# A graph layer's edge stage: a gather waits for the sums three groups back instead of seven

## The chip, the core and the metric

The kernel runs on one core of a Trainium2 chip. Its engines are TensorE (PE in the profile; PEld is its weight load), VectorE (DVE), ScalarE (ACT), GpSimd (POOL) and SyncE (SP). Each runs its own list of instructions in order, and they meet only at semaphores. The metric is device time of one execution in microseconds (us).

## What is computed

A graph attention layer and a mixture of eight experts, one behind the other, over 2500 nodes of 512 features. The change touches only the first. Cut to what matters:

```python
# nodes: layernorm of x; 40000 edges (src, dst), sorted by dst
h = nodes @ W + b_w                        # 2500 x 512
s_dst, s_src = h @ a[:512], h @ a[512:]
e = leaky_relu(s_dst[dst] + s_src[src] + b_a, 0.2)
w = exp(e)
denom = segment_sum(w, dst)
out = segment_sum((w / denom[dst])[:, None] * h[src], dst)
x = x + out                                # then the experts
```

## The kernel before

**Stages.** First `h` is made and stored to a table in DRAM (`node_table`), a row of 516 f32 for each node: two halves of features, a one (which sums to the denominator) and the node's score. Then comes the edge stage, which this case is about, from about 92 to 574 us of the profile. Then come the second layernorm, the routing and the experts.

**The edge stage.** The 40000 edges are cut into chunks of 128 (an edge on each partition), and four chunks are a group: 79 groups, numbered here from 0 to 78, the last with one chunk. As edges are sorted by target, a group's targets nearly always lie in one tile of 128 nodes; where they reach into a second tile the group has an *extra*, a second pass for that tile. 19 of the 79 groups have one: 3, 7, 11 and so on up to 71, then 76. A group goes through these steps:

1. POOL issues four indirect DMAs (L506), one for each chunk, which fetch 128 rows of the table into slot `g % 8` of the ring `rows`.
2. ACT waits for all four (`got`) and for DVE to have read the low exponentials before, and makes eight activations of 128x128 (L951): `E`, and a second set in PSUM.
3. DVE takes the larger of the two (`Wt`, L1217, after the short `lane`, L1222) and masks it in four instructions into `S` (L1228), which releases the semaphore `S_ok`. Then, in its own program order, it adds the finished sums of group g-2 to `acc` (L1235), for which it waits for `agg_ok`.
4. PE multiplies `S` with `rows` (L705, function `sums`), 16 matmul records of 128x257 for a full group; the last one raises `agg_ok`. The PSUM banks alternate between two groups.
5. An extra repeats steps 2 to 4 from the same slot: ACT follows at once with another eight activations (`E`, `E2x`), DVE weighs them behind its add of group g-2, and PE sums them behind the group's own sums. They do not raise `agg_ok` but a semaphore of their own.

PE, ACT and DVE run this in a loop of eight groups (`RING`) with branches around the extras; at the loop's edge they load the words that tell a group's tiles. POOL's list is written out for all 79 groups. `S` has four slots of its own, `rows` eight.

**What the change touches.** `gather(g)` on POOL. POOL has nothing else to do from the first gather to the last, and nothing follows on it until `acc_ok`, the end of the stage.

Of the kernel before, what the change touches and what calls it, by code (L numbers as in the profile page):

```python
# [20 lines left out]
def gnn_moe_kernel(nc, x, src, dst, gnn_W, gnn_b_w, gnn_a, gnn_b_a, Wg, bg, W1, b1, W2, b2, out):  # L21
# [7 lines left out]
    CJ = -(-CH // P)  # L29
    GC = 4  # L30
    RING = 8
    U = 4
    NG = -(-CH // GC)
    GC_LAST = CH - GC * (NG - 1)
    NGR = -(-NG // RING) * RING
    SR = U
    BACK = 2
# [20 lines left out]
    with ExitStack() as ctx:  # L58
# [3 lines left out]
        def sem(name):  # L62
            return ctx.enter_context(nc.semaphore(name))
# [23 lines left out]
        def sg(name, shape, dt, into=None):  # L87
            top[0] += size(shape, dt)
            return (into or ctx).enter_context(nc.sbuf_tensor(name, shape, dt))
# [17 lines left out]
        top[0] = ring  # L107
        rows = sg("rows", [P, RING, GC, ROW], F32, first)
        assert layer_end <= top[0]
# [160 lines left out]
        st_row = [[sem(f"st_row{s}{j}") for j in range(2)] for s in range(2)]  # L270
        got = [sem(f"got{r}") for r in range(RING)]
        exp_ok, id_ok = sem("exp_ok"), sem("id_ok")
        max_ok = [sem("max_ok0"), sem("max_ok1")]
        S_ok, agg_ok = sem("S_ok"), sem("agg_ok")
# [76 lines left out]

        def window_words(eng, regs, i, back=0, each=RING):

            eng.load(regs, window[0:1, bass.ds(each * i + BACK - back, len(regs))])
# [133 lines left out]
        def _(pool):  # L488
# [11 lines left out]

            def gather(g):

                if g >= RING - 1:
                    pool.wait_ge(agg_ok, g - RING + 2)
                for c in range(GC if g < NG - 1 else GC_LAST):
                    nc.gpsimd.indirect_dma_start(  # L506
                        out=rows[:, g % RING, c, :], out_offset=None, in_=table,
                        in_offset=bass.IndirectOffsetOnAxis(ap=srcT[:, GC * g + c:GC * g + c + 1], axis=0))\
                        .then_inc(got[g % RING], 16)
# [5 lines left out]
            for g in range(NG):  # L515
                gather(g)
# [574 lines left out]
        def _(dve):  # L1091
            regs = [dve.alloc_register(f"dve_window{k}") for k in range(U + BACK)]
            n_dv = [0]
# [121 lines left out]
            def largest(q, n=GC):  # L1215

                return nc.vector.scalar_tensor_tensor(out=Wt[:, q, 0:n, :], in0=E1[:, q, 0:n, :], scalar=FINITE,  # L1217
                                                      in1=(E2x[:, 0, 0:n, :] if q == 2 else ps_E2[:, 0:n, :]), op0=ALU.min, op1=ALU.max)
# [6 lines left out]
            def masked(q, w, n=GC):  # L1225

                for c in range(n):
                    m = nc.vector.scalar_tensor_tensor(  # L1228
                        out=S[:, w, c, :], in0=ps_id[:, :], scalar=lane[:, w, c:c + 1],
                        in1=Wt[:, q, c, :], op0=ALU.is_equal, op1=ALU.mult)  # L1230
                return m
# [43 lines left out]
            def step_of_group(g, r, i, first=False, chunks=GC):  # L1275

                word, word_before = dve.snap(regs[r + BACK]), dve.snap(regs[r])
                dve.wait_ge(exp_ok, g + 1)
                if not (first and r < 2):
                    dve.wait_ge(S_ok, g - 1)  # L1280
                tile = dve.snap(tile_in(word))
                lanes(r % SR, g, tile)
                largest(r % 2, chunks).then_inc(max_ok[r % 2], 1)
                dve.wait_ge(max_ok[r % 2], U // 2 * i + r // 2 + 2)
                masked(r % 2, r % SR, chunks).then_inc(S_ok, 1)
                if not (first and r < 2):
                    add_group(g - 2, r % 2, word_before, first and r < 3)
                extras(g, None if first and r < 2 else g - 1, word, chunks)
# [17 lines left out]
            dve.wait_ge(edges_ok, 2)  # L1306
            window_words(dve, regs, 0, BACK, U)
            for r in range(U):
                step_of_group(r, r, 0, first=True)
            with dve.Fori(1, NG // U) as i:  # L1310
                window_words(dve, regs, i, BACK, U)
# [248 lines left out]
```

## Time and profile before

| | us |
|---|---|
| three runs | 866.72, 867.32, 867.40 |
| median | 867.32 |
| span of the profiled execution | 861.7 |
| what lies around the span, against the median | 5.6 |
| edge stage within the span | about 92 to 574 |

The span runs from the first to the last instruction of the profiled execution. Busy time of an engine is the time that its instructions take, without register and semaphore work. The granted clock (PEclk) is 1.00 when TensorE runs at 2.4 GHz and 0.50 at 1.2 GHz.

### The profile page before, as it was taken

What the parts mean: (1) busy time and instruction counts of PE and PEld (TensorE: products, weight loads), DVE (VectorE), ACT (ScalarE), POOL (GpSimd) and SP (SyncE); (2) the same over time, 40 slices, a digit from 0 to 9 for tenths busy, and PEclk for the clock granted to TensorE, in tenths of its full rate; (3) what the DMA queues carried; (4) which work ended last, traced back from release to release, by engine and by line L of the source; (5) the groups of instructions that cost most, each with busy time, mean ns of one, the idle gap of its engine ahead of it and who ended that gap; (6) DMA issues with size and microseconds to landing.
All of it is one profiled execution on the core that took longest, in us unless ns stands there. A gap on an engine that the chain in (4) does not pass through costs nothing.

```text
span 861.7 us, 14833 instructions
## 1 busy us (share of the span) xinstructions
PE 696.6 (81%) x3260; PEld 553.6 (64%) x3261; DVE 457.2 (53%) x1232; ACT 415.4 (48%) x1134; POOL 457.3 (53%) x530
## 2 busy tenths in 40 slices
PE   4999355879888787879788888959889999999960
PEld 3777245657766666667676767845547787888840
DVE  5998223555555555556465555668485433333320
ACT  4443442545545554536455545618754444545430
POOL 5000575666666666666666666310105677777750
PEclk9999687998989899989999898988988999999995
DMA  5342576666666666666656666407993577777768
GB/s 197 117 155 92 156 213 164 172 188 168 186 181 174 178 177 182 186 171 183 189 166 184 176 179 179 118 27 283 334 380 127 104 131 131 135 131 135 130 91 250
DMA packets 58299, 146.96 MB, mean 171 GB/s; under 512 B 8868, under 2 KB 18708, under 8 KB 57880
## 3 DMA queue, kind: packets, MB, share of 16 engines
q0 software_dynamic: 35216, 106.84, 50.6%
q1 hardware_dynamic: 22968, 37.16, 12.3%
q10 hardware_dynamic: 80, 2.56, 1.0%
q8 instruction: 14, 0.23, 0.1%
q14 instruction: 21, 0.17, 0.1%
HBM read 118.17 MB, written 33.47 MB: 176 GB/s over the span
## 4 chain that ended last, share of the span: by engine, by line
PE 40%; issue 19%; DVE 11%; DMA 11%; ACT 4%; POOL 4%; POOLq 2%; DVEq 2%; another core or an unknown queue 2%; ACTq 1%; SPq 1%
PE ps L705 30%; DMA result<-y,si 8%; PE ps L659 3%; POOL rows L506 2%; DMA x_all<-in_x_dram 2%; ACT E L951 2%; ACT ps L951 2%; PE ps L844 1%; DVE Wt L1217 1%; PE ps L785 1%; DVE S L1228 1%; DVE acc L1235 1%; PE ps L755 1%; POOL xg L593 1%
## 5 line engine op out<-in xcount | busy, mean ns | idle before, releaser
L705 PE MATMUL ps<-rows,S 128*128 128x257 f32 x1556 | 383.4, 404 | 98.7 <-issue 83.9
L506 POOL DMA_INDIRECT rows<-node_table,srcT x313 | 301.8, 964 | 234.4 <-issue 83.8
L705 PEld LDWEIGHTS ps<-rows,S 128*128 128x128 f32 x1556 | 312.3, 202 | 169.6 <-issue 121.3
L951 ACT ACTIVATE E<-sdst_b,rows 128x128 f32 x389 | 124.0, 389 | 236.2 <-DVE Wt L1217 120.7
L1235 DVE TENSOR_TENSOR acc<-acc,ps 128x514 f32 x99 | 68.0, 687 | 116.1 <-remote 77.6
L1228 DVE SCALAR_TENSOR_TENSOR S<-ps,lane,Wt 128x128 f32<-128x128 f32 x389 | 109.6, 345 | 4.4 <-issue 0.8
L951 ACT ACTIVATE ps<-sdst_b,rows 128x128 f32 x313 | 96.2, 351 | 2.0 <-issue 2.0
L844 PE MATMUL ps<-W_e,xgT 128*128 x352 | 83.4, 380 | 0.0
L602 POOL DMA_INDIRECT result<-y,si x44 | 70.4, 1601 | 11.4 <-issue 7.1
L1222 DVE TENSOR_TENSOR lane<-dstT,node_id 128x4 f32 (+1 forms) x98 | 16.1, 164 | 111.5 <-issue 77.0
L844 PEld LDWEIGHTS ps<-W_e,xgT 128*128 128x128 f32 x352 | 63.4, 190 | 6.9
L659 PE MATMUL ps<-Wb,xT 128*128 128x512 f32 x240 | 59.1, 403 | 2.5 <-DVE dstT L1184 1.4
L858 PE MATMUL ps<-W_hi,hidT 128*128 x176 | 55.6, 437 | 3.0 <-DVE hidT L1512 2.8
L1058 ACT ACTIVATE act_h<-hid 128x256 f32<-128x256 f32 x44 | 18.4, 418 | 77.2 <-DVE hid L1519 67.2
L1529 DVE TENSOR_TENSOR y_b<-ps,b_b 128x512 f32<-128x512 f32 x44 | 30.4, 692 | 46.4 <-PE ps L858 39.4
L659 PEld LDWEIGHTS ps<-Wb,xT 128*128 128x128 f32 x240 | 45.6, 194 | 12.6 <-DVE dstT L1184 1.6
L1217 DVE SCALAR_TENSOR_TENSOR Wt<-E,ps 128x512 f32<-128x512 f32 (+1 forms) x79 | 53.3, 675 | 0.0
L593 POOL DMA_INDIRECT xg<-xn_table,gi x44 | 48.1, 1094 | 8.1 <-issue 4.6
L1519 DVE TENSOR_TENSOR hid<-ps,b_b 128x256 f32<-128x256 f32 x44 | 18.7, 424 | 55.1 <-PE ps L844 51.3
L551 POOL COPY si<-dst_row 128x1 int32 (+1 forms) x45 | 31.9, 709 | 19.0 <-DVE need L1503 11.9
L858 PEld LDWEIGHTS ps<-W_hi,hidT 128*128 128x128 f32 x176 | 32.6, 188 | 11.8 <-issue 5.9
L548 POOL COPY gi<-src_row 128x1 int32 (+1 forms) x45 | 9.7, 215 | 54.0 <-DVE src_row L1458 35.9
(203 smaller groups left out, 678.8 us busy)
## 6 DMA issues: line engine op xcount, KB each, us to landing
W_e<-in_L_ffn_W_dram SPq DMA_DIRECT2D x16, 512.0 KB, 8.5
node_table<-rows SPq DMA_DIRECT2D x20, 258.0 KB, 2.7
result<-acc SPq DMA_DIRECT2D x20, 256.0 KB, 2.5
xn_table<-xn SPq DMA_DIRECT2D x20, 256.0 KB, 2.2
rows<-node_table,srcT POOLq DMA_INDIRECT x313
x_all<-in_x_dram SPq DMA_DIRECT2D x19, 256.0 KB, 3.1
out_dram<-result SPq DMA_DIRECT2D x1, 2500.0 KB, 16.7
out_dram<-result ACTq DMA_DIRECT2D x1, 2500.0 KB, 18.4
```

The costliest lines, as they stand in the source:

```text
L506: nc.gpsimd.indirect_dma_start(out=rows[:, g % RING, c, :], out_offset=None, in_=table, in_offset=bass.IndirectOffsetOnAxis(ap=srcT[:, GC ...
L551: nc.gpsimd.tensor_copy(si[:, r, :], dst_row[:, bass.ds(i, 1)]).then_inc(si_ok, 1)
L593: nc.gpsimd.indirect_dma_start(out=xg[:, r, :], out_offset=None, in_=xn_table, in_offset=bass.IndirectOffsetOnAxis(ap=gi[:, r, :], axis=0) ...
L602: nc.gpsimd.indirect_dma_start(out=result, out_offset=bass.IndirectOffsetOnAxis(ap=si[:, (r - LAG) % YR, :], axis=0), in_=y[:, (r - LAG) % ...
L659: m = pe.matmul(ps_h[s][j][:, :], xT[:, s, a, k, j * P:(j + 1) * P], Wb[:, b, k, :], start=(n == 0), stop=(n == 3 * KT - 1))
L705: m = pe.matmul(ps_agg[q][:, a, 0:HALF], S[:, w, c, :], rows[:, r, c, a * HALF:(a + 1) * HALF], start=(c == 0), stop=(c == n - 1))
L844: m = pe.matmul(ps_hid[1 - s][:, 0:F], xgT[:, 1 - s, k * P:(k + 1) * P], W1_e[:, bass.ds(e, 1), k, :].rearrange("p e f -> p (e f)"), start ...
L858: m = pe.matmul(ps_y[s][:, :], hidT[:, s, a, k * P:(k + 1) * P], W[:, bass.ds(e, 1), k, :].rearrange("p e d -> p (e d)"), start=(c == 0), ...
L951: m = nc.scalar.activation(e[:, c, :], sdst_b[:, bass.ds(tile * P, P)], ACT.Exp, bias=bias, scale=scale)
L1217: return nc.vector.scalar_tensor_tensor(out=Wt[:, q, 0:n, :], in0=E1[:, q, 0:n, :], scalar=FINITE, in1=(E2x[:, 0, 0:n, :] if q == 2 else p ...
L1228: m = nc.vector.scalar_tensor_tensor(out=S[:, w, c, :], in0=ps_id[:, :], scalar=lane[:, w, c:c + 1], in1=Wt[:, q, c, :], op0=ALU.is_equal, ...
L1235: nc.vector.tensor_tensor(a, a, ps_agg[q][:, :, 0:HALF], ALU.add).then_inc(count, 1)
```

## The change

A new constant `AHEAD = 3`, and the wait ahead of a gather. Before, the gather of group g waited until the sums of groups 0 to g-7 were done; now it waits for those of groups 0 to g-3, and it does so from group 3 on instead of from group 7. The ring keeps its eight slots; no instruction is added or taken out apart from four more waits (groups 3 to 6), and nothing else changes.

```diff
     GC = 4
     RING = 8
+    AHEAD = 3
@@
             def gather(g):
 
-                if g >= RING - 1:
-                    pool.wait_ge(agg_ok, g - RING + 2)
+                if g >= AHEAD:
+                    pool.wait_ge(agg_ok, g - AHEAD + 1)
                 for c in range(GC if g < NG - 1 else GC_LAST):
```

## Rows read from the trace of the kernel before

**Rows 1.** The page: costliest group; count, busy us, mean ns, idle before

```profile
L705 PE MATMUL ps<-rows,S 128*128 128x257 f32 x1556 | 383.4, 404 | 98.7 <-issue 83.9
```

**Rows 2.** Waits, 150 to 550 us: who for whom, total us, times, longest

```profile
PE ps L705 <- issue: 62.1, 69, 2.4
...
PE ps L705 <- DVE acc L1235: 2.6, 4, 0.8
```

**Rows 3.** Windows: POOL's gathers, then DVE's `Wt` instructions, up to a time

```profile
92.00:343.40 251.40, 164.98 (x172) 0.88 0.66 180
...
92.00:344.40 252.40, 32.74 (x48) 0.89 0.66 181
```

**Rows 4.** Timeline of POOL at 343 us: start, us, idle before

```profile
343.44 0.94 POOL L506 DMA_INDIRECT rows<-node_table,srcT  x1 [1.26 <-remote]
```

**Rows 5.** Timeline of DVE: `Wt` of groups 7, 47 (and its extra), 48 and 71

```profile
157.16 0.68 DVE L1217 SCALAR_TENSOR_TENSOR Wt<-E,ps 128x512 f32<-128x512 f32 x1
...
391.54 0.68 DVE L1217 SCALAR_TENSOR_TENSOR Wt<-E,ps 128x512 f32<-128x512 f32 x1
...
395.37 0.69 DVE L1217 SCALAR_TENSOR_TENSOR Wt<-E,E2x 128x512 f32<-128x512 f32 x1
396.09 1.13 DVE L1228 SCALAR_TENSOR_TENSOR S<-ps,lane,Wt 128x128 f32<-128x128 f32 x4
...
399.28 0.68 DVE L1217 SCALAR_TENSOR_TENSOR Wt<-E,ps 128x512 f32<-128x512 f32 x1
...
533.23 0.68 DVE L1217 SCALAR_TENSOR_TENSOR Wt<-E,ps 128x512 f32<-128x512 f32 x1
```

**Rows 6.** Timeline of the stage's start, groups 0 and 1

```profile
92.24 1.15 POOL L506 DMA_INDIRECT rows<-node_table,srcT  x1 [78.54 <-DMA node_table<-rows]
...
97.47 0.94 POOL L506 DMA_INDIRECT rows<-node_table,srcT  x1 [0.30 <-issue]
...
104.71 8.80 PE L705 MATMUL ps<-rows,S 128*128 128x257 f32 x32 [15.06 <-issue]
...
105.15 1.28 ACT L951 ACTIVATE E<-sdst_b,rows 128x128 f32 x4 [2.65 <-DMA rows<-node_table,srcT]
...
107.85 0.68 DVE L1217 SCALAR_TENSOR_TENSOR Wt<-E,ps 128x512 f32<-128x512 f32 x1
```

**Rows 7.** Timeline of POOL: the gather that sums released

```profile
296.25 0.94 POOL L506 DMA_INDIRECT rows<-node_table,srcT  x1 [1.35 <-PE ps L705]
```

**Rows 8.** Windows, L705 alone: PE and PEld busy (records), clock, DMA share, GB/s

```profile
294.88:295.30 0.42, 0.42 (x2) 0.33 (x1) 0.50 0.77 177
200.20:241.00 40.80, 33.58 (x149) 27.86 (x148) 1.00 0.68 184
357.80:404.90 47.10, 39.86 (x160) 32.14 (x160) 0.93 0.66 180
...
379.83:388.60 8.77, 5.64 (x17) 4.03 (x16) 0.81 0.60 168
392.17:395.60 3.43, 3.43 (x17) 3.00 (x16) 1.00 0.75 181
```

**Rows 9.** Timeline, 382 to 384 us: PE and DVE

```profile
382.71 0.38 PE L705 MATMUL ps<-rows,S 128*128 128x257 f32 x1 [1.73 <-issue]
383.43 0.16 DVE L1222 TENSOR_TENSOR lane<-dstT,node_id 128x4 f32 x1 [6.12 <-issue]
```

**Rows 10.** Windows, L705 alone: blocks of groups 3 and 7, and 72 to 78

```profile
137.90:143.70 5.80, 5.77 (x17) 4.77 (x18) 0.64 0.63 162
...
159.85:163.50 3.65, 3.65 (x18) 3.21 (x18) 1.00 0.75 213
...
541.20:571.80 30.60, 29.33 (x134) 24.95 (x133) 1.00 0.24 69
```

**Rows 11.** DMA queues, 200 to 500 us: packets, MB, share

```profile
q0 software_dynamic: 16264, 53.69, 65.5%
q14 instruction: 1, 0.01, 0.0%
```

## The prediction

> **What bounds the kernel now.** I read the page first. TensorE's edge matmuls are its costliest group, 1556 records and 383.4 us busy, all in the edge stage [rows 1]. Then the waits: from 150 to 550 us the PE idles 62.1 us on "issue" in 69 pieces of at most 2.4 us, and 2.6 us on DVE; it never waits for rows to land [rows 2]. "Issue" means that its own list of instructions came slowly, which I come back to. So the PE and the pace of its instructions set the stage.
>
> How far ahead do gathers run? Up to 343.40 us POOL had issued 172 gathers, which is groups 0 to 42, and up to 344.40 DVE had made 48 `Wt`, which is groups 0 to 38 and nine extras [rows 3]. The first gather of group 43 starts at 343.44 [rows 4], when the PE, which follows DVE, can be on group 38 at most. A block (the 16 records of a group or an extra) takes 3.4 us at full clock [rows 8]. Under the new rule this gather would wait for the sums of group 40. So the wait will bind for each group; the change does what it says.
>
> The period: `Wt` of group 7 starts at 157.16 and that of group 71 at 533.23 [rows 5]. Eight loops of eight groups take 376.07 us, 47.0 each. In such a loop there are ten blocks, 160 records, which occupy the PE for 39.9 of 47.1 us [rows 8].
>
> **The change, part by part.** Nothing is added that costs by itself: a wait on POOL, behind which only POOL's later gathers stand, and POOL has 5.2 us of issuing for a group (92.24 to 97.47) [rows 6] against 47.0 / 8 = 5.9 now. What changes is that data no longer lies ready when ACT wants it. A chain closes: sums of g-3, gather of g, landing, exponentials, `Wt`, mask, sums of g. Its pieces:
>
> *From the first gather to the end of the sums.* At the start of the stage nothing lies ready and the trace shows just this. Group 1: gather at 97.47, ACT starts at 105.15 after waiting for the rows, `Wt` at 107.85, and the PE row of groups 0 and 1 ends at 104.71 + 8.80 = 113.51 [rows 6]. That is 16.0 us: 7.7 to the landing, 2.7 for ACT, 5.7 for mask and sums.
>
> *From the end of the sums to the next gather.* The one plain case: POOL at 296.25 after an idle of 1.35 that the PE ended [rows 7]. The block's last record begins at 294.9 and lasts to 295.3, as the short window with two records around it shows [rows 8]. So 0.98 us. The chain from sums to sums three groups on is 17.0 us, 5.67 a group. By itself this is less than 5.9.
>
> *The extra.* It stands every fourth group, between the sums of groups 3 and 4, 7 and 8, and so on. Since its rows are those of its group, its work starts at once and can't be spread. Take group 47: `Wt` at 391.54, the extra's `Wt` at 395.37, its mask done at 396.09 + 1.13 = 397.22, 5.68 after the group's own `Wt` [rows 5]. The group's sums end 5.66 after its `Wt` (113.51 - 107.85), so the extra's sums can't start sooner than these end; two blocks of 3.5 with their starts make 7.3 us from the sums of group 3 to those of group 4. At the loop's edge DVE sets it: `Wt` of 47 to `Wt` of 48 is 399.28 - 391.54 = 7.74 us [rows 5].
>
> Four groups then cost one chain and one extra, not four thirds of a chain: from the sums of 0 by the chain to those of 3 (17.0), and by the extra to those of 4 (7.3 or 7.7). Eight groups: 34.0 + 7.3 + 7.7 = 49.0 us, against 47.0 now. This is the floor of the new period, 2.0 us above the old with nothing else in it. The old one holds slow stretches as well.
>
> *The slow stretches.* The block of group 44 takes 8.77 us with 16 records of its own (the seventeenth is the end of the block before), the block of group 46 takes 3.43 [rows 8]. At 382.71 one record comes 1.73 us after the one before; DVE's `lane` of group 45 comes after 6.12 us of "issue" in the same stretch [rows 9]. Such a block comes once in each loop, at the group that is 4 past a multiple of eight, and then some smaller ones. Group 4 of a loop is on the new chain, right behind an extra, where the PE has no slack to hide it. What is it worth? Nothing if an idle PE lets the list of instructions catch up; up to 12 us if the smaller ones land on the chain too (47.1 - 10 x 3.5 = 12 us is all that the PE loses in a loop now). I take the one long block in full, 8.8 - 3.4 = 5.4, as it starts on both engines when neither was waiting, and the smaller ones as hidden. The period becomes 54.4 us, 7.4 more. Eight loops: +59 us.
>
> Here the Trainium skill has a rule, in "Runtime: NRT & Kernel Launch", section "Instruction fetch mechanics": the list of instructions is fetched in order in blocks, and a taken branch whose target isn't in the two blocks held makes the engine wait for a fetch by DMA. By it the stretches belong to places in the loop and stay, which gives the sum above; a catch-up during waits would give the first rival's. The trace bears it out in part: the places do recur, but from 200 to 500 us the instruction queues show one packet against 16264 of the gathers [rows 11], so no fetch by DMA is seen at each of them.
>
> *The ends of the stage.* At the start, the sums of group 3 end at 143.3 at the earliest (from 137.90 16 records at mixed clock) [rows 10]; group 6 then starts its gather at 144.3 and group 7, behind the sums of 4 (a block of 3.5 and an extra of 3.5 later), at 151.3, so its sums end at 167.3. They end at 163.5 now [rows 10]: +4. At the stage's end, groups 72 to 78 now take 571.8 - 541.2 = 30.6 us behind the sums of 71 [rows 10]. By the chain: extra and 72 (7.3), 73 (3.5), the chain to 76 (17.0), extra and 77 (7.3), and 1 for the short 78: 36. So +6. Together +10.
>
> After the stage nothing is different: POOL's next work already waited for `acc_ok`.
>
> **Sum.** 59 + 10 = +69 us. The profiled span of 861.7 becomes 931; the median stands 5.6 above the span, so 867.3 becomes 936 us.
>
> **Rivals.**
>
> A, *the slow stretches vanish in the waits.* For it: most of these stretches are short, and the PE will pause ahead of most blocks. Against it: the long one comes right behind an extra, where neither PE nor DVE would be waiting. Then the period is 49.0: 8 x 2.0 + 10 = +26, 893 us.
>
> B, *the clock falls.* The PE would be busy 35 of 54 us, with a pause of about 2 us ahead of most blocks. The block of 44 had a clock of 0.81, but from 200.20 to 241.00 it is 1.00 throughout, with 40.8 - 33.6 = 7.2 us of pauses in between [rows 8]. If it falls in half the six blocks on the chain of a loop (0, 3, 4, 7 and two extras), each adds 3.4: +10 a loop, +80 in all, 1016 us.
>
> The Trainium skill speaks for B, in "TensorE: Matmul & The Clock Gate", section "HAM oscillation": short bursts of matmuls, each behind a wait for a DMA, run at the low clock again and again. By it the time would go towards 1016; the clock of 1.00 over 40 us with pauses in it disagrees so far, but there the pauses are rarer than they will be.
>
> C, *faster: fewer gathers ahead ease the slow stretches for everyone.* The gathers' queue has a share of 65.5% [rows 11] and could be what slows the engines' lists. If they vanish with it and the chain is shortened too, time is gained. It decides where the chain falls below 16.0 us (then 32.0 + 15.0 = 47.0). At 15.0 the period is 45.0: -16 + 10 = -6, 861 us. Against it: of the 7.7 to the landing, 4 are POOL's issuing of four gathers, which doesn't shrink, and group 1 was measured where just one group was ahead of it. At about 15.8 the whole would come to no change.
>
> **How the numbers follow.** About 0.2% (1.7 us) is what a measurement of this kernel can tell. Chances: the forecast 0.61 (its own range 915 to 989: from half the long block, 49.0 + 2.7, to all 12 us on the chain, 61.0), A 0.20, B 0.12, C 0.07, of which 0.04 faster and 0.03 the same. Slower 0.93. The range of 8 in 10 runs from 888, just under A, to 990: it leaves out C and most of B.
>
> **What the profile after would show.** POOL before the first gather of each group idle, released by the PE; ACT's `E` waiting for DMA or "remote" where it now waits for DVE; PE waits between blocks of about 2 us; `Wt` to `Wt` over eight groups 54 us (49 would be A, over 60 B, 47 or less C); at groups 4 of a loop still a block of 8 to 9 us; the stages behind 574 us shifted and otherwise equal. The prediction would be wrong if a gather lands much sooner than 7.7 us after its issue, if the extra overlaps with the next group more than DVE's order allows, or if the slow stretches move or multiply when the engines run in step.

## The result and the profile after

| us | before | with the change |
|---|---|---|
| median | 867.36 (4 runs) | 878.06 (4 runs, 876.02 to 879.09) |
| ratio | | 1.0112, 95% interval 1.0097 to 1.0127 |
| span of the profiled execution | 861.7 | 877.4 |

The change makes the kernel 1.1% slower, 10.7 us. The forecast was 69 us, with 888 to 990 as its range; the direction was right and the size was not. One point on the time itself: the profiled execution after took 879.09 us for its span of 877.4, so 1.7 us lie around a span, not 5.6. The profiled execution of before was therefore some 4 us quicker than its median, and the two profiles differ by 15.7 us where the medians differ by 10.7.

The page after, the two costliest groups of the edge stage (against [rows 1]; lines are one higher in the changed file):

```profile
L706 PE MATMUL ps<-rows,S 128*128 128x257 f32 x1556 | 377.2, 402 | 122.2 <-DVE acc L1236 74.1
L507 POOL DMA_INDIRECT rows<-node_table,srcT x313 | 298.6, 954 | 266.7 <-PE ps L706 93.1
```

POOL now waits for the PE, as the change asks. The PE waits more than before and for another reason. Waits of the PE, 150 to 570 us, against [rows 2]:

```profile
PE ps L706 <- DVE acc L1236: 68.3, 33, 3.4
PE ps L706 <- issue: 20.2, 10, 3.0
PE ps L706 <- DVE S L1229: 5.6, 3, 2.9
```

"Issue" falls from 62.1 to 20.2 us and DVE rises from 2.6 to 73.9. (These are waits for `S`, as the mask's semaphore and that of the add stand side by side ahead of a block.) The label "issue" needs care here: in both of these traces many semaphore events are not recorded (the experiments come back to it), and an idle time whose end has no event goes to "issue". A measure that needs no semaphore is the idle time inside a block, between two of its 16 records, where the PE waits for nobody. Pieces of over 0.3 us, counted in the trace from `Wt` of group 7 to that of group 71, add up to 45.9 us before (51 pieces) and to nothing after. So the slow stretches of the PE are gone: the block of group 44, which took 8.77 us with 16 records [rows 8], now looks like any other. The blocks at this place of the eight loops (groups 12, 20 and so on to 68) took 8.8 to 11.4 us before and take 3.6 to 3.7 after. Windows, L706 alone; the columns are those of [rows 8]; the blocks of groups 39, 44 and 51, then most of the stage:

```profile
349.05:352.70 3.65, 3.57 (x17) 3.15 (x18) 1.00 0.69 186
...
380.10:383.70 3.60, 3.60 (x17) 2.85 (x16) 1.00 0.73 193
423.35:429.70 6.35, 6.29 (x16) 5.07 (x17) 0.54 0.60 166
150.00:550.00 400.00, 308.94 (x1284) 253.59 (x1284) 0.94 0.61 169
```

The block of group 51 ran at a clock of 0.54 and took 6.3 us: rival B, in single blocks.

The period, from the timeline of DVE, `Wt` of groups 7 and 71, against [rows 5]:

```profile
148.39 0.68 DVE L1218 SCALAR_TENSOR_TENSOR Wt<-E,ps 128x512 f32<-128x512 f32 x1
...
546.74 0.68 DVE L1218 SCALAR_TENSOR_TENSOR Wt<-E,ps 128x512 f32<-128x512 f32 x1
```

398.35 / 8 = 49.8 us a loop, against 47.0. So the 15.7 us of the spans are: group 7 comes 8.8 us sooner (157.16 to 148.39), eight loops cost 22.3 more, and about 2 are left for the end of the edge stage and all behind it.

The chain that the forecast wrote down, in the timeline of all engines from 335 to 374 us: group 39 with its extra, group 40, then the gathers of 42 and 43 and the block of 43:

```profile
335.84 0.94 POOL L507 DMA_INDIRECT rows<-node_table,srcT  x1 [2.02 <-PE ps L706]
...
343.75 1.28 ACT L952 ACTIVATE E<-sdst_b,rows 128x128 f32 x4 [4.56 <-DMA rows<-node_table,srcT]
...
346.55 0.68 DVE L1218 SCALAR_TENSOR_TENSOR Wt<-E,ps 128x512 f32<-128x512 f32 x1
...
349.13 10.66 PE L706 MATMUL ps<-rows,S 128*128 128x257 f32 x48 [3.26 <-DVE acc L1236]
...
353.72 0.94 POOL L507 DMA_INDIRECT rows<-node_table,srcT  x1 [1.37 <-PE ps L706]
...
360.06 0.94 POOL L507 DMA_INDIRECT rows<-node_table,srcT  x1 [1.65 <-PE ps L706]
...
373.11 8.06 PE L706 MATMUL ps<-rows,S 128*128 128x257 f32 x36 [0.84 <-DVE acc L1236]
```

From gather to the end of the sums: 7.9 to the landing, 2.8 to `Wt`, 2.6 to the first record, 3.7 for the block, 17.0 in all where the forecast had 16.0. The release is shorter than forecast where POOL is ready: the 48 records (group, extra, group 40) end at 359.79 and the gather of 43 starts at 360.06, 0.3 us later. The gather of 42 comes about 1 us behind the sums of 39, as forecast. In e6, the same kernel on another chip, the release is 0.27 us behind most groups and the chain 17.0 to 17.4 us where the clock stays up; there the two errors nearly cancel.

### The profile page after: what moved, and what is told of

It reads as the page before. It is cut to its first block, busy times and chain, and to the rows that moved or that the text cites. A ratio compares the mean times of both kernels' runs of the same rounds, so it can differ in the third digit from the quotient of the medians.

```text
span 877.4 us, 14833 instructions
## 1 busy us (share of the span) xinstructions
PE 688.0 (78%) x3260; PEld 549.3 (63%) x3261; DVE 453.8 (52%) x1232; ACT 415.5 (47%) x1134; POOL 454.1 (52%) x530
## 3 DMA queue, kind: packets, MB, share of 16 engines
q0 software_dynamic: 35216, 106.84, 48.5%
## 4 chain that ended last, share of the span: by engine, by line
PE 33%; issue 18%; DVE 14%; DMA 12%; POOL 10%; ACT 5%; DVEq 2%; POOLq 1%; another core or an unknown queue 1%; ACTq 1%; SPq 1%
PE ps L706 15%; POOL rows L507 9%; PE ps L845 6%; DMA rows<-node_table,srcT 5%; PE ps L859 4%; DMA result<-y,si 3%; PE ps L660 3%; ACT ps L952 2%; DVE acc L1236 2%; DVE S L1229 2%; ACT E L952 2%; DVE Wt L1218 2%; DMA x_all<-in_x_dram 2%; DMA xg<-xn_table,gi 2%; PE ps L835 2%
## 5 line engine op out<-in xcount | busy, mean ns | idle before, releaser
L706 PE MATMUL ps<-rows,S 128*128 128x257 f32 x1556 | 377.2, 402 | 122.2 <-DVE acc L1236 74.1
L507 POOL DMA_INDIRECT rows<-node_table,srcT x313 | 298.6, 954 | 266.7 <-PE ps L706 93.1
L706 PEld LDWEIGHTS ps<-rows,S 128*128 128x128 f32 x1556 | 309.1, 202 | 190.1 <-DVE S L1229 92.8
L594 POOL DMA_INDIRECT xg<-xn_table,gi x44 | 48.1, 1094 | 8.1 <-issue 5.5
L1520 DVE TENSOR_TENSOR hid<-ps,b_b 128x256 f32<-128x256 f32 x44 | 18.7, 424 | 50.7 <-PE ps L845 47.3
```

The costliest lines, as they stand in the source:

```text
L507: nc.gpsimd.indirect_dma_start(out=rows[:, g % RING, c, :], out_offset=None, in_=table, in_offset=bass.IndirectOffsetOnAxis(ap=srcT[:, GC ...
L594: nc.gpsimd.indirect_dma_start(out=xg[:, r, :], out_offset=None, in_=xn_table, in_offset=bass.IndirectOffsetOnAxis(ap=gi[:, r, :], axis=0) ...
L706: m = pe.matmul(ps_agg[q][:, a, 0:HALF], S[:, w, c, :], rows[:, r, c, a * HALF:(a + 1) * HALF], start=(c == 0), stop=(c == n - 1))
```

## The experiments

The kernel before does not take the same time everywhere, and that turned out to be the main finding. The experiments ran in five sets, each on another chip, with the kernel before beside them; its medians were 787.6, 786.9, 868.6, 862.2 and 865.0 us, and within a set its times agree within 1%. So each run must be read against the kernel before of its own set. The text speaks of two kinds of chip, with and without slow stretches. As no chip served twice, and that of the first measurement isn't on record, it isn't shown that the chip is the cause and not something else that differed from set to set.

The loop time is that from `Wt` of group 7 to `Wt` of group 71, divided by eight, in the timeline of DVE of each run. "Idle in blocks" is the measure from above, for the same eight loops. "Signals" tells how many of the landing signals of the gathers the trace recorded: each gather raises its semaphore in 16 steps, however many rows it fetches, so 313 gathers make 5008 and 103 make 1648. e3, e4, e5, e7, e8, e10, e12 and e14 are one execution each.

| run | before beside it | time | `Wt` of 7 | loop, us | idle in blocks, us | signals |
|---|---|---|---|---|---|---|
| before (first profile) | | 867.36 | 157.16 | 47.0 | 45.9 | 1295 of 5008 |
| the change (first profile) | 867.36 | 878.06 | 148.39 | 49.8 | 0 | 2120 of 5008 |
| e1, four ahead | 787.58 | 788.03 | 140.65 | 40.0 | 0 | 5008 of 5008 |
| e2, five ahead | 787.58 | 787.73 | 138.66 | 40.1 | 0 | 5008 of 5008 |
| e3, one gather of four | 787.58 | 749.82 | 139.45 | 35.6 | 0 | 1648 of 1648 |
| e4, half of the PE's sums | 787.58 | 785.81 | 139.55 | 40.0 | 0 | 5008 of 5008 |
| e5, before again | 786.87 | 789.56 | 139.84 | 40.1 | 0 | 5008 of 5008 |
| e6, the change again | 786.87 | 880.76 | 151.65 | 49.4 | 0 | 5008 of 5008 |
| e7, two ahead | 786.87 | 1146.43 | 166.47 | 77.7 | 0 | 5008 of 5008 |
| e8, the change, one gather of four | 868.63 | 809.51 | 151.71 | 41.1 | 0 | 1389 of 1648 |
| e9, four ahead again | 868.63 | 860.33 | 144.01 | 47.8 | 21.0 | 1382 of 5008 |
| e10, one gather of four again | 868.63 | 763.50 | 154.02 | 35.6 | 0 | 1290 of 1648 |
| e11, a pause on POOL | 862.15 | 873.02 | 158.43 | 48.3 | 30.0 | 1627 of 5008 |
| e12, half of the PE's sums again | 862.15 | 861.48 | 157.33 | 47.6 | 0 | 1278 of 5008 |
| e13, five ahead again | 862.15 | 857.74 | 147.67 | 47.0 | 44.2 | 1367 of 5008 |
| e14, a quarter of the rows | 864.96 | 867.27 | 161.10 | 47.0 | 51.4 | 906 of 5008 |
| e15, four ahead, then seven | 864.96 | 864.31 | 142.77 | 49.0 | 42.6 | 1325 of 5008 |

The last column divides the runs as the time of the kernel before does: where it takes 787 us every signal is recorded, where it takes 860 to 870 us it is 18% to 84% of them. In the second kind the labels "issue" and "remote" ("remote": a release whose origin the profile doesn't show) are therefore rough. It also names a rival to all theories below, which no run tests: every time on record comes with a span and a granted clock, so from an execution that was recorded, and the recording itself may be what holds the engines up on these chips.

The theories: 1, the slow stretches come where PE and DVE run without waiting, and waits hide them; 2, they come with long unbroken runs of POOL's gathers; 3, the forecast's, they belong to places in the code and stay.

### e1 and e2: four and five groups ahead

```diff
-    AHEAD = 3
+    AHEAD = 4        # e2: 5
```

> A gather waits for the sums four groups back instead of three. The chain from sums to sums (17.0 us) then covers four groups, and a loop of eight groups costs at least two chains and, one group further, an extra: 2 x 17.0 + 7.5 / 5 x 8 is under 42 us, so POOL's issuing sets the floor, 8 x 5.0 to 5.2 = 40 to 42 us a loop. Theory 1 (the slow stretches come where PE and DVE run through their lists without having to wait; a wait lets the lists catch up): PE is busy 35 of 42 us and still waits, so few stretches, 42 to 44 us a loop, 30 to 40 us faster than the kernel before. Theory 2 (the stretches come at the end of long unbroken runs of POOL's indirect DMAs, 8 to 12 in a row, and end when POOL pauses): the runs are as long as in the kernel before, the stretches are back, 46 to 48 us a loop, within 8 us of the kernel before. Theory 3 (they belong to places in the loop's code, as in the prediction): also 46 to 48 us.

> A gather waits for the sums five groups back. The chain does not bind. Theory 1: like the kernel before in steady state, since data lies ready again: 46 to 47 us a loop, within 5 us of before, perhaps a few us gained at the start of the stage. Theory 2: the same as before, within 5 us. Theory 3: the same. This run is the middle of the series 3, 4, 5, 7 and shows where the time turns.

Ratios to the kernel before of the set: 1.0011 (0.9988 to 1.0034) and 0.9996 (0.9981 to 1.0012). The loop is 40 us, but so it is for the kernel before (e5): there are no slow stretches on this chip. The expectations about them are untested here. What both runs do show is that from four groups on the chain does not bind: POOL's issuing sets the pace, as the floor of 40 to 42 us said.

### e3 and e4: light gathers, light PE

```diff
# e3: from group 8 on only chunk 0 is gathered
-                for c in range(GC if g < NG - 1 else GC_LAST):
+                for c in range(GC if g < RING else 1):
# e4: the PE sums two chunks of four
+                n = min(n, 2)
                 for c in range(n):
```

In e3 ACT's wait on `got` counts to match.

> The kernel before, but from group 8 on only the first of the four chunks of a group is gathered; the other three keep the rows of eight groups earlier. It leaves out three quarters of the gathers. ACT, DVE and PE do all their work, and nothing waits for data. Theory 1 (stretches where PE and DVE never wait) and theory 3 (places in the code): the stretches stay, the period of eight groups stays at 45 to 47 us. Theory 2 (unbroken runs of POOL's indirect DMAs, or their traffic): the stretches vanish and the period falls to the PE's own, 10 blocks of 3.5 us plus the loop's edge, 37 to 39 us, 60 to 80 us faster in all.

> The kernel before, but the PE sums only the first two of four chunks of each group and extra, so a block takes 1.7 instead of 3.5 us. It leaves out half of the sums. POOL then sets the pace with unbroken runs of gathers, and ACT, DVE and PE wait for data. Theory 1: no stretches, 40 to 42 us a loop. Theory 2: the runs of indirect DMAs are longer than ever, so PE, DVE and ACT show instructions 0.7 us apart through most of the stage, and POOL itself is slowed: 46 us a loop or more. Theory 3: the stretches stay where they were but are partly hidden: 42 to 44 us.

Without stretches to see, these tell the bounds: with half of the PE's work the loop stays at 40.0 us, with a quarter of the gathers it falls to 35.6, the PE's own ten blocks. So POOL bounds the kernel before on such a chip.

### e5 and e6: both kernels again, side by side

> The kernel before, unchanged, for its profile beside the next run. In the last call the kernel before took 787.6 us on its chip, 80 us less than in the first measurement, and the changed variants there showed no slow stretch on the PE at all. Theory 4: the slow stretches are a matter of the chip or of its surroundings, not of the kernel's code (against theory 3) and not of unbroken runs of indirect DMAs alone (against theory 2). Where the time is near 787, the trace has no stretch of PE or DVE instructions 0.7 us apart outside the extras, and POOL issues without a pause, a group each 5.0 us, 40 us a loop; where it is near 867, it looks like the first trace, 47 us a loop.

> The change, unchanged. The chain of the prediction (two chains of 17.0 and two extras of 7.3 and 7.7 us: 49.0 us a loop; 48.0 to 48.3 measured where the clock did not fall) does not depend on slow stretches. On a chip without them the kernel before has 40 us a loop, so the change costs 8 us a loop and about 8 at the end, nothing at the start: +65 to +80 us, 855 to 870 us, against 787 before; the changed kernel is then nearly as fast as on the first chip (878), as the stretches had left it anyway. On a chip with them: 876 to 880 against 867, as first measured. Rival (the change helps or costs the same everywhere): a ratio of 1.01 on any chip.

Here the change costs 12%: 880.76 against 786.87, ratio 1.1203 (1.1170 to 1.1236), 94 us, more than the 65 to 80 expected. Between the two profiles lie 91.7 us: 75.0 are the eight loops (9.4 each, where the expectation had 8), 5 come behind them, and 11.8 stand ahead of group 7, where "nothing at the start" was expected: the chain binds there too, from group 3 on. The kernel before, `Wt` of groups 7 and 71 and its waits from 150 to 450 us:

```profile
139.84 0.68 DVE L1217 SCALAR_TENSOR_TENSOR Wt<-E,ps 128x512 f32<-128x512 f32 x1
...
460.33 0.68 DVE L1217 SCALAR_TENSOR_TENSOR Wt<-E,ps 128x512 f32<-128x512 f32 x1
...
ACT E L951 <- DMA rows<-node_table,srcT: 74.3, 38, 3.5
POOL rows L506 <- issue: 73.4, 241, 0.3
```

POOL never waits for anything but its own next issue (at most 0.3 us), and ACT waits for rows, where in the first profile data lay ready. The changed kernel:

```profile
151.65 0.68 DVE L1218 SCALAR_TENSOR_TENSOR Wt<-E,ps 128x512 f32<-128x512 f32 x1
...
547.07 0.68 DVE L1218 SCALAR_TENSOR_TENSOR Wt<-E,ps 128x512 f32<-128x512 f32 x1
```

Its loop of 49.4 is within 0.4 of the first profile's 49.8. So the changed kernel is the same on both kinds of chip, set by the chain, and the kernel before is the one that differs, 40.1 or 47.0. The small first ratio is a difference of two losses. The rival of e6, a ratio of 1.01 everywhere, is refuted, and so far theory 4 of the expectation to e5 holds.

### e7: two groups ahead

```diff
-    AHEAD = 3
+    AHEAD = 2
```

> A gather waits for the sums two groups back. The same chain of 17.0 us then covers two groups. Four groups cost two chains, or one extra edge and one and a half chains, whichever is longer: 34.0 us or 7.5 + 25.5 = 33.0, so 68 us a loop against 48 to 49 with three. That is 79/8 x 19 = +190 us against the change: about 1050 to 1070 us. Rival (the landing gets much shorter when fewer gathers are under way): under 60 us a loop, under 990 us.

The chain's direction and more: 77.7 us a loop, 1146 us. Of the 9.7 us beyond 68, the clock is the one cause that shows. The window of the PE's edge matmuls, columns as in [rows 8]:

```profile
150.00:750.00 600.00, 345.57 (x1229) 280.40 (x1229) 0.75 0.39 109
```

A mean clock of 0.75, against 0.94 with three ahead. In the timeline of the PE four blocks of each loop take longer than the usual 3.65 us, together by 8.5 to 10.1 us, which is nearly the whole of the 9.7. The wait of the next gather is long enough here for the clock to fall again and again. That is rival B, true at two groups and a minor matter at three. The Trainium skill's rule of "TensorE: Matmul & The Clock Gate", section "HAM oscillation", describes this run; at three groups it was too strong.

### e8: the change with light gathers

The edit of e3 on the changed kernel.

> The change, but from group 8 on only the first of the four chunks of a group is gathered; the other three keep older rows. It leaves out three quarters of the gathers. It tests a term of the chain: of the 16.0 us from the first issue to the end of the sums, 3 x 1.25 = 3.75 are the issuing of three more gathers on POOL. By the chain, a loop falls from 48.1 (24.07 for four groups, as measured) to 2 x (17.0 - 3.75 + 7.1) = 40.7 us, or a little more where the clock falls. Total on a chip without slow stretches: 880 - 9 x 7.5 = 810 to 820 us. Rival (the bytes on the way are what takes time, so a quarter of them lands much earlier): under 38 us a loop. Rival (the wait itself or the semaphores cost, not the issuing): 46 to 48 us a loop.

41.1 us a loop for the expected 40.7, and 809.51 us, just under the 810 to 820. The term "of the 7.7 us to the landing, 4 are POOL's issuing" holds: take three gathers out and the chain loses about their 3.75 us. Both rivals are out. The expected total was for a chip without slow stretches; this one has them (868.63 beside it), and with light gathers they do not show.

### e9 and e13: four and five ahead, where the kernel before takes 860 to 870

> Four groups ahead, unchanged from the earlier run, in the hope of a chip with slow stretches (before near 867). There: theory 1 (waiting lets the lists catch up) 42 to 44 us a loop in place of 47.0, 820 to 840 us, theory 2 (long unbroken runs of indirect DMAs) and theory 3 (places in the code) within 8 us of 867. On a chip without them: 786 to 790 as before.

> Five groups ahead, unchanged from the earlier run. On a chip with slow stretches: between four (860 against 868.6) and seven (868.6) groups, 862 to 868 us. On a chip without: 786 to 790.

Four ahead: ratio 0.9903 (0.9878 to 0.9929). Five ahead: 0.9935 (0.9915 to 0.9955), 857.74 us, 4 us under the expected range, beside a kernel before of 862.15. Both are a gain, and neither makes a loss on the other kind of chip (e1, e2). But the loop is 47.8 and 47.0, not the 42 to 44 of theory 1: the gain lies ahead of group 7, which comes 13.2 and 9.5 us sooner than in the first profile of before (there is no trace of the kernel before from these two chips). With four ahead the PE still loses time to "issue" (waits of PE, 150 to 540 us):

```profile
PE ps L706 <- issue: 34.9, 34, 2.5
PE ps L706 <- DVE acc L1236: 25.8, 20, 4.0
```

The idle time in blocks tells it without the label: 45.9 us with seven groups ahead, 44.2 with five, 21.0 with four, none with three. The stretches fade as the wait tightens, while the chain's cost grows.

### e10: light gathers, where the kernel before takes 868.6

> The kernel before with a quarter of the gathers from group 8 on, unchanged from the earlier run. On a chip with slow stretches: if they stay with so few gathers (period 45 to 47 us a loop, total near 860), the gathers' traffic and POOL's runs have no part in them; if they vanish (37 us a loop, near 760), they have. On a chip without them: 750 us and 35.6 us a loop, as in the earlier run.

35.6 us a loop, to the tenth the value of e3: no stretches. Theory 3 falls here. The code of PE, DVE and ACT is the same, place by place, and runs at full pace. The 13.7 us between e10 and e3 lie ahead of group 7 (`Wt` at 154.02 and 139.45), while all gathers of groups 0 to 7 are still issued, 32 in a row: there e10 has a slow stretch as the kernel before has one.

### e11: a pause on POOL after each group

```diff
                         .then_inc(got[g % RING], 16)
+                nc.gpsimd.memset(pause[:, :], 0.0).then_inc(pause_ok, 1)
+                pool.wait_ge(pause_ok, g + 1)
```

> The kernel before, seven groups ahead, but POOL makes a small memset (128x384) after each group's four gathers and waits for it, a pause of about 0.6 us; POOL's own pace is then 5.6 us a group or 45 us a loop. On a chip with slow stretches (before near 868). Theory 1 (the lists catch up where engines wait for data): with POOL at 45 us a loop against the PE's 35, the engines come to wait for data, but so they would at 40 us, where the stretches hold; theory 1 alone expects 45 to 47 us, 0 to -18 us. Theory 2 (unbroken runs of indirect DMAs): no run is longer than four, the stretches vanish, 45 us a loop, 845 to 852 us. If the average traffic counts and not the runs, it is close to that of the kernel before (45 against 47 us a loop) and nothing changes: 862 to 870. On a chip without stretches: 787 + 9.9 x 4.8 = 830 to 838 us.

Ratio 1.0114 (1.0085 to 1.0144): slower, and 48.3 us a loop. The timeline of POOL shows the pause in place, and the one of the PE a slow stretch in spite of it:

```profile
360.71 0.95 POOL L508 DMA_INDIRECT rows<-node_table,srcT  x1 [0.30 <-issue]
361.66 0.43 POOL L512 MEMSET pause<- 128x384 f32 x1
362.36 0.95 POOL L508 DMA_INDIRECT rows<-node_table,srcT  x1 [0.27 <-issue]
```

```profile
365.14 0.38 PE L709 MATMUL ps<-rows,S 128*128 128x257 f32 x1 [0.63 <-issue]
365.89 0.46 PE L709 MATMUL ps<-rows,S 128*128 128x257 f32 x1 [0.37 <-issue]
367.30 0.47 PE L709 MATMUL ps<-rows,S 128*128 128x257 f32 x1 [0.96 <-issue]
```

Records 0.7 and 1.4 us apart where 0.22 is normal. No run of gathers is longer than four, so long unbroken runs aren't needed for the stretches, and theory 2 in that form falls. (That they make them worse is seen in e15.) The pause is short, 1.65 us from gather to gather instead of 1.25; a longer one wasn't tried.

### e12: half of the PE's sums, where the kernel before takes 862

> The kernel before, with the PE summing two chunks of four, unchanged from the earlier run. On a chip with slow stretches: POOL's 40 us a loop would set the pace and PE has much slack. If waiting lets the lists catch up (theory 1), 41 to 43 us a loop, 800 to 815 us, no stretches on the PE. If the gathers' traffic alone makes them (theory 2), DVE and POOL keep them and the loop stays above 45 us, 840 us or more. On a chip without: 786.

861.48 us and 47.6 us a loop: half of the PE's matmuls are gone and the time does not move. Waits of the PE, 150 to 540 us:

```profile
PE ps L706 <- DVE acc L1236: 109.1, 28, 8.1
PE ps L706 <- issue: 50.6, 21, 8.6
PE ps L706 <- DVE S L1229: 21.8, 17, 1.8
```

The PE has 131 us of waits for DVE, but the loop is not shorter, for DVE is slow itself, and that is where the stretches are now (waits of DVE, 150 to 550 us, then one of them in its timeline):

```profile
DVE lane L1223 <- issue: 122.3, 47, 6.8
...
318.51 0.16 DVE L1223 TENSOR_TENSOR lane<-dstT,node_id 128x4 f32 x1 [6.70 <-issue]
```

A part of the 122.3 can be waits for ACT whose event isn't recorded, but not all. In this gap the trace has DVE's register instructions, which wait for nobody: four of them from 312.7 to 317.6 take 0.70 us each, with up to 1.4 us between them, where one takes 0.04 to 0.08 otherwise. From `Wt` of 7 to that of 71, 90 of 832 such instructions on DVE take over 0.4 us, against 44 in the first profile of before, one in that of the change, and none in any run beside a kernel before of 787. (ACT has 24 of 544 here, 10 before and still 16 with the change, so the slowness is not quite gone there.) That the instructions themselves take longer is more than a list that comes slowly.

Theory 1 expected 41 to 43 us, so waiting on the PE alone does not cure the stretches. It also corrects the forecast's first sentence: the PE's matmuls were not what set the pace of the kernel before.

### e14: a quarter of the rows, all gathers

```diff
+                p = P if g < RING else P // 4
-                        out=rows[:, g % RING, c, :], out_offset=None, in_=table,
+                        out=rows[0:p, g % RING, c, :], out_offset=None, in_=table,
```

The index column is cut to the same partitions.

> The kernel before, but from group 8 on each of the four gathers of a group fetches only 32 of its 128 rows; the other rows keep older data. It leaves out three quarters of the rows but none of the gathers: as many instructions on POOL, a quarter of the bytes and descriptors. It divides what the run with one gather of four took away. On a chip with slow stretches (before 862 to 869): if the bytes or descriptors on the way make them, they vanish, and the loop falls to 40 us or less (POOL's issuing, if it costs the same for 32 rows), 790 to 805 us; if the issuing itself on POOL makes them, they stay, 46 to 48 us a loop, 855 us or more. On a chip without: 40 us a loop and 787 us if the issuing time does not depend on the rows, down to 35.6 us and 750 us if it does.

867.27 us, 47.0 us a loop, as the kernel before, with a quarter of the bytes. The DMA view from 150 to 550 us (queue, packets, MB, share), then the page's group of POOL:

```profile
q0 software_dynamic: 8640, 17.85, 19.1%
```

```profile
L507 POOL DMA_INDIRECT rows<-node_table,srcT x313 | 275.8, 881 | 263.9 <-issue 89.0
```

The share fell from 65.5% [rows 11] to 19.1%, the packets of these 400 us from 21640 in the first profile of before to 8640, and the stretches stayed. So the bytes and the load of the DMA engines have no visible part in them. With e10, they go with the number of gathers. Whether that means their issuing on POOL or what each gather brings whatever its size, its 16 landing signals and their records among it, these runs don't tell apart.

### e15: four ahead up to group 11, then seven

```diff
-                if g >= RING - 1:
-                    pool.wait_ge(agg_ok, g - RING + 2)
+                ahead = 4 if g < 12 else RING - 1
+                if g >= ahead:
+                    pool.wait_ge(agg_ok, g - ahead + 1)
```

> Four groups ahead up to group 11, then seven as before. With four and five ahead the gain on a chip with slow stretches lay at the start of the stage (13.2 and 9.5 us by the Wt of group 7) and not in the loop. If that is so, this one starts as early as four ahead and has the 47.0 us loop of seven: 850 to 858 us there, a ratio of 0.985 to 0.992. Rival (the gain moves, since the gathers must catch up later and the stretches come then): 860 to 868. On a chip without stretches: 786 to 790.

Ratio 0.9996 (0.9978 to 1.0015): the rival holds. `Wt` of groups 7 and 15:

```profile
142.77 0.68 DVE L1218 SCALAR_TENSOR_TENSOR Wt<-E,ps 128x512 f32<-128x512 f32 x1
...
203.85 0.68 DVE L1218 SCALAR_TENSOR_TENSOR Wt<-E,ps 128x512 f32<-128x512 f32 x1
```

The start is 14.4 us sooner than in the first profile of before, and the first loop then takes 61.1 us where the later ones take 47.2 to 47.3. The gain is given back by the time group 15 is reached. The timeline shows where: from group 12 on the wait is looser, so POOL issues 20 gathers in a row, from 156.6 to 181.3 us, and DVE and PE stand still from 170 to 185:

```profile
185.15 0.69 DVE L1236 TENSOR_TENSOR acc<-acc,ps 128x514 f32 x1 [15.98 <-remote]
185.99 14.61 PE L706 MATMUL ps<-rows,S 128*128 128x257 f32 x54 [16.04 <-DVE acc L1236]
```

What this `acc` waited for, the sums of group 9, had ended at 165.9. So a long unbroken run of gathers does bring a long stop, though e11 shows that stretches need no such run.

## Why the prediction was wrong

**The chain: right.** Two chains and two extras were to cost 49.0 us a loop. The loops in which the clock does not fall, in the first profile after and in e6, take 48.0 to 48.5. Its inner terms hold too: e8 took the issuing out and got 41.1 for 40.7.

**The step that failed: "I take the one long block in full, 8.8 - 3.4 = 5.4, as it starts on both engines when neither was waiting, and the smaller ones as hidden."** It measured 0: no block at these places takes more than 3.7 us after. The old period of 47.0 held about 7 us that the new one does not: on chips without stretches the kernel before needs 40.1. The forecast added to the chain's cost a loss that the change takes away. Instead of +7.4 us a loop there were +2.8: 8 for the chain beyond 40.1, 1.7 for falls of the clock (49.8 less 48.1), and 7 back.

**The start: wrong in sign.** Forecast +4, measured -8.8 by group 7. The forecast took the end of the sums of group 3, 143.3, from the old trace as if nothing could move it. A slow stretch stood ahead of it: from 115.8 to 132.4 us twelve register instructions of ACT take 0.7 us each, and `Wt` of groups 3 and 4 lie 21.7 us apart. After the change three instructions are slow, the two `Wt` lie 6.5 us apart, the sums of group 3 end at 129.9, and the gather of group 7 starts at 137.2 and not at 151.3.

**The end: near.** Forecast +6 for the groups behind 71; from `Wt` of 71 to the last gather's sums it is +4.6 (533.23 to 571.36 before, 546.74 to 589.44 after, by the start of the last record).

**Rival A** named the right thing, the stretches vanish, and got 0.20. Its 893 is 14 too high for the profiled 879.1: the start is 12.8 too high (+4 for -8.8), all behind group 71 is 4 too high, the time around the span 4 too high, and the loops are 6 too low (49.8 for 49.0 a loop). **Rival B** was there and small, 1.7 us a loop instead of 10. **Rival C** is refuted: its condition, a loop below 47, would have needed a chain under 16.0, and the chain is 17.0 to 17.4. Its first half, that fewer gathers ahead ease the stretches, was right; with four and five ahead (e9, e13) it even makes the kernel 1.0% and 0.6% faster. Its reason, the load of the gathers' queue, is refuted by e14.

**"The PE and the pace of its instructions set the stage"**: the first half was wrong (e12), and the second right only in that the engines ran slowly. That "issue" means a slow list was taken from the label, which also takes in waits without a recorded event. The stretches should have been a term of their own with its own question: what makes them?

The rule of the Trainium skill that stood beside this step ("Runtime: NRT & Kernel Launch", section "Instruction fetch mechanics") made them a matter of branches and places in the loop. e10 disagrees: the same branches in the same places cost nothing once POOL issues one gather of four.

**What stays open.** Why the stretches vanish under the change, though POOL still issues four gathers in about 6.2 us, as against 5.9 before and 6.0 in e11 where they stay. One reading fits the averages of all runs: on these chips 32 gathers take at least about 47 us, and the stretches are what holds the engines back to that pace. No run there with four gathers a group averages less: 47.0 before, with five ahead and with a quarter of the rows, 47.2 in the later loops of e15, 47.6 with half of the sums, 47.8 with four ahead, 48.3 in e11, where POOL's own pace would be 45. The chain of the change asks for 48.0 or more by itself, so nothing is left to hold back. By this reading the chain and the stretches never add up; the longer of the two counts. It was made after the runs, and none tests it: a pause on POOL that makes its own pace 49 us a loop, without a chain, would. Why some chips show the stretches and others don't isn't known either, nor whether they would show in an execution that nobody records.

## What to carry to other kernels

A wait that limits how far loads run ahead closes a chain; write it out from the first load to the release, divide by the groups it spans, and hold it against the period that the kernel would have *without* its present losses (40 here), not against the one that it has (47). Idle time labelled "issue" is not a fixed cost of the code, and may not even be a slow list: ask what else it depends on, and whether the trace has all its semaphore events, before carrying it over into a sum. And where a ratio is small because two large terms cancel, it can be 1.01 on one chip and 1.12 on another, as it was here; five groups ahead was as fast as seven or faster on both, and three was slower on both.

## What the runs showed of the hardware

The same kernel took 787 us on two chips and 862 to 869 us on three others and in the first measurement, 40.1 and 47.0 us a loop, with records of the PE 0.7 or 1.4 us apart in the slow stretches and register instructions of DVE of 0.70 us. The trace of the first measurement holds 1295 of the gathers' 5008 landing signals, the traces of 787 us hold all of them. In the slow stretches the number of POOL's indirect DMAs counts, not their size: with all gathers at a quarter of the rows 47.0 us a loop at 19.1% DMA share, with one gather of four 35.6. An indirect DMA of 32 rows occupies POOL nearly as long as one of 128: the mean of all 313 is 881 ns (the first 32 of them full) against 964. At two groups ahead the PE, with long waits between blocks, ran at a mean clock of 0.75.
